# A recommendation tower on one core: wider warm-up products, a wait moved, transposes regrouped and five gather holds removed

## The reference, cut to what matters

```python
e = stack([tbl_f[ids[:, f]] for f in range(26)], axis=1)      # 512 samples, 26 tables, 128 floats a row
combined = concatenate((dense[:, None, :], e), axis=1)         # 27 slots a sample
inter = einsum('bfd,bgd->bfg', combined, combined)             # 27 x 27 products a sample
z = concatenate((dense, inter[:, iu, ju]), axis=1)             # 351 pairs above the diagonal
h = concatenate([z, dense], axis=1)                            # 607 columns
h = maximum(h @ W_top1 + b_top1, 0)                            # 512
h = maximum(h @ W_top2 + b_top2, 0)                            # 256
y = h @ W_top3                                                 # 1 number a sample
```

## Time and profile before

| | |
|---|---|
| Median of 3 runs | 124.61 us (124.29 to 125.33) |
| Span of the profiled execution, first to last instruction | 123.0 us |
| The profiled execution's own time | not given apart from its span; the median is 1.6 us above the span |
| PE busy, PEld busy | 104.2 us, 87.9 us |
| VectorE, ScalarE, GpSimd busy | 65.4, 48.1, 65.7 us |
| DMA | 13.51 MB, mean 110 GB/s |
| Chain that ended last | PE 83%, "issue" 13%, VectorE 2%, ScalarE 1% |

### The profile page before, as it was taken

One profiled execution on the slowest core, in us unless ns is written; L12 is line 12 of the kernel. 1 busy time (PEld: TensorE's weight loads), 2 busy tenths in 40 slices (PEclk: granted clock), 3 DMA queues, 4 the chain that ended last, 5 costly groups with the idle time before them and its releaser, 6 DMA issues.

```text
span 123.0 us, 3436 instructions
## 1 busy us (share of the span) xinstructions
PE 104.2 (85%) x1516; PEld 87.9 (71%) x1516; DVE 65.4 (53%) x110; ACT 48.1 (39%) x81; POOL 65.7 (53%) x66
## 2 busy tenths in 40 slices
PE   6999999999999999962178996289995299998993
PEld 6787888888888888831067895177992278996991
DVE  2599999999899996820001742105540106451411
ACT  4542979197794931300000462002541102730321
POOL 3887888579878887877500887503778305000000
PEclk9999999999999999999555999756999558999999
DMA  3799999999211112121200111200112100000000
GB/s 57 236 400 365 402 398 408 410 392 368 80 43 45 45 43 48 44 63 43 64 5 5 43 43 43 64 0 0 45 43 64 43 0 20 23 0 0 0 0 1
DMA packets 3949, 13.51 MB, mean 110 GB/s; under 512 B 1315, under 2 KB 1317, under 8 KB 3302
## 3 DMA queue, kind: packets, MB, share of 16 engines
q1 hardware_dynamic: 2018, 9.48, 20.5%
q0 software_dynamic: 1920, 3.94, 11.2%
q10 hardware_dynamic: 4, 0.00, 0.0%
HBM read 13.42 MB, written 0.00 MB: 109 GB/s over the span
## 4 chain that ended last, share of the span: by engine, by line
PE 83%; issue 13%; DVE 2%; ACT 1%
PE bank L365 17%; PE prod L408 13%; PE bank L414 13%; PE prod L365 12%; PE bank L374 7%; PE bank L504 6%; PE prod L433 4%; PE bank L321 4%; PE bank L325 3%; PE bank L445 2%; DVE inter_s L585 1%; PE bank L438 1%; PE prod L421 1%; PE bank L421 0%; DVE xT L575 0%
## 5 line engine op out<-in xcount | busy, mean ns | idle before, releaser
L313 POOL DMA_INDIRECT emb<-in_tbl,ids_sb x60 | 65.0, 1083 | 38.3 <-PE prod L408 19.3
L522 DVE TENSOR_SCALAR mask<-ids_h,ids_sb 128x1024 fp32r<-128x1024 int16 (+1 forms) x48 | 31.5, 699 | 2.2 <-issue 0.8
L408 PE MATMUL prod<-xT 128*27 128x27 f32 x1024 | 16.8, 215 | 14.7 <-issue 14.2
L408 PEld LDWEIGHTS prod<-xT 128*27 128x27 f32 x1024 | 13.6, 128 | 18.8 <-issue 17.4
L585 DVE STREAM_TRANSPOSE inter_s<-prod 128x288 f32<-128x288 f32 (+1 forms) x8 | 4.6, 611 | 26.3 <-PE prod L408 26.3
L365 PE MATMUL bank<-mask,high 128*128 128x512 f32 x46 | 15.2, 393 | 0.0
L365 PE MATMUL bank<-mask,low 128*128 128x512 f32 x46 | 15.0, 390 | 0.0
L414 PE MATMUL bank<-pairs,w_sb 117*128 117x128 f32 x96 | 12.7, 282 | 0.1
L414 PEld LDWEIGHTS bank<-pairs,w_sb 117*128 117x128 f32 x96 | 11.6, 191 | 0.7 <-ACT pairs L696 0.5
L531 DVE TENSOR_TENSOR low<-table,high 128x1024 fp32r<-128x1024 f32 (+1 forms) x9 | 11.7, 1301 | 0.0
L374 PE MATMUL bank<-ident,emb 128*128 128x128 f32 x60 | 10.5, 310 | 0.9 <-issue 0.9
(11 more groups left out here) (55 smaller groups left out, 118.1 us busy)
## 6 DMA issues: line engine op xcount, KB each, us to landing
table<-in_resident SPq DMA_DIRECT2D x3, 1024.0 KB
w_sb<-in_weights SPq DMA_DIRECT2D x1, 1792.0 KB
table<-in_resident SPq DMA_DIRECT2D x1, 1280.0 KB
table<-in_resident SPq DMA_DIRECT2D x4, 256.0 KB
emb<-in_tbl,ids_sb POOLq DMA_INDIRECT x60
ids_h<-in_other_ids SPq DMA_DIRECT2D x1, 896.0 KB
table<-in_resident SPq DMA_DIRECT2D x1, 640.0 KB
ids_h<-in_pair_ids SPq DMA_DIRECT2D x1, 256.0 KB
```

The lines of the kernel that those rows point to most:

```text
L313: nc.gpsimd.indirect_dma_start(out=rows(t, c), out_offset=None, in_=gathered[c], in_offset=bass.IndirectOffsetOnAxis(ap=ids_sb[:, i:i + 1] ...
L408: mm = nc.tensor.matmul(prod[SLOT_PITCH * q:SLOT_PITCH * q + SLOTS, i, 0:SLOTS], x, x, start=True, stop=True)
L522: nc.vector.tensor_scalar(made(step)[:, 0:n, :], ids_h[:, 2 * b:2 * b + n, :], col_sb[:, row:row + 1], None, ALU.is_equal).then_inc(s_mask, 1)
```

## The change

- `keep_busy` multiplies 128 columns instead of 64, and its second use has 5 calls instead of 7.
- A semaphore `s_warmed` is counted behind that second use, and ScalarE's cast of pair 1 waits for it instead of for `s_used` at 1.
- Between the halves of the products TensorE transposes groups 0 and 1 of the next tile. The dense parts 0 and 1 stand behind the second half in every pass, pass 1 too; nothing else stands there.
- The five holds of GpSimd behind the lookups are gone: before gather 10 of tile 2 and before gathers 0, 4, 9 and 13 of tile 3 (counted from 0). The four holds within the lookups stay, and the waits for the buffers (`s_tr`).

```diff
-WARM_UP, WARM_KEEP = 4, 7
-WARM_COLUMNS = 64
+WARM_UP, WARM_KEEP = 4, 5
+WARM_COLUMNS = 128
@@
+        s_warmed = sem("s_warmed")
@@ hold
                 if (t, i) == (2, 6):
                     pool.wait_ge(s_used, first_step[5] + 3)
-                if (t, i) == (2, 10):
-                    pool.wait_ge(s_prod, 1)
-                if (t, i) == (3, 0):
-                    pool.wait_ge(s_l1, 2)
-                if (t, i) == (3, 4):
-                    pool.wait_ge(s_prod, 2)
-                if (t, i) == (3, 9):
-                    pool.wait_ge(s_l1, 4)
-                if (t, i) == (3, 13):
-                    pool.wait_ge(s_prod, 3)
@@
             def keep_busy(n):
                 for _ in range(n):
-                    nc.tensor.matmul(half_bank[1][:, 0:WARM_COLUMNS], warm, warm[:, 0:WARM_COLUMNS], start=True, stop=True)
+                    mm = nc.tensor.matmul(half_bank[1][:, 0:WARM_COLUMNS], warm, warm[:, 0:WARM_COLUMNS],
+                                          start=True, stop=True)
+                return mm
@@
-            keep_busy(WARM_KEEP)
+            keep_busy(WARM_KEEP).then_inc(s_warmed, 1)
             look_up_first()
@@ the tile loop
                 products(range(MATMULS // 2))
-                turn_next(p, (0,))
-                with nc.tensor.If(p < 2):
-                    dense_part(slice(0, P), (0, 1))
+                turn_next(p, (0, 1))
                 products(range(MATMULS // 2, MATMULS)).then_inc(s_prod, 1)
                 samples = bass.ds((p - 1) * P, P)
                 with nc.tensor.If(p > 1):
 
                     result(p - 1)
-                    dense_part(samples, (0, 1))
-                turn_next(p, (1,))
+                dense_part(samples, (0, 1))
@@ upper_parts
-                    act.wait_ge(s_used, 1)
+                    act.wait_ge(s_warmed, 1)
```

## The result

The changed kernel takes 139.59 us (median of 6 runs, 137.93 to 140.25) against 124.79 us for the kernel before beside it (6 runs, 124.29 to 125.33): ratio 1.112, 95% interval 1.106 to 1.118. It is slower by 15 us. The profiled execution has a span of 138.1 us and took 139.92. Every median here is over all executions of a kernel, but every ratio compares only executions outside a second, slower state that any kernel falls into now and then, so a ratio can differ by some tenths of a per cent from that of the two medians beside it.

A forecast was written before the change was run, and what follows sets the result against it. TensorE was taken to bound it nearly throughout, starved 17.3 us beside gathers. 100.3 + 38.7 - 5.5 - 0.9 = 132.6 us span, plus 1.6 for the median, 134.2, said as 134; range 121 to 139.

The forecast's parts named there:

- Gathers starve TensorE: Products of passes 1 to 3: gathers cause the starved stretches, 17.3 us, argued from three gather ends just before TensorE's return.
- The order of events: Pass 1's first half starves to 67 or 68 us, its second stretches, pass 2's first starves, pass 3 doesn't.
- the late effect: Rival: starvation begins only some time after a restart, so pass 1's second half escapes; span 126.5, forecast 128; chance 0.11.
- the faster case: Rival: held gathers' bursts starve passes 2 and 3, so only pass 1 pays; span 117, forecast 118.5; chance 0.20.
- no change: Rival: the stretches belong to the loop, not the gathers; 123 to 125 us, forecast 124; chance 0.13.
- The reserve: Beside gathers TensorE has 50 matmuls at full rate before creeping, refilled when gathers pause; in pass 1's second half, 19 left.
- the upper bound, +3 to +5: If the reserve counts from the gathers' issue, pass 1's second half waits out all eight gathers: +3 to +5 us.
- The return: Pass 1's first half: TensorE returns at 67.7 us, after the last gather's end at 65.9.
- The front: Start of the lookups: wider products raise the clock before the first lookup matmul, pair 0 ends at 14.5, gain 1.2 us.
- the allowance: Lookups: alongside gathers TensorE can steadily issue 4.0 matmuls a us; the lookups need 4.4 and were said to fit.
- The low clock: Layer 1 after pass 1's products takes 1 us more at the low level; two turned groups between halves 2.05 us.
- The sum: Span 132.6 us, +9.6: pass 2's products end at 100.3, plus 38.7, minus 5.5 and 0.9 saved in pass 3 and later.

The follow-up runs named there:

- run 6: The kernel before without the 26 gathers from gather 4 of tile 2 on: 106.21 us against 125.72.
- run 7: The kernel before with the same 26 loads as plain transfers of fixed rows from GpSimd's queue: 104.63 us against 125.72, ratio 0.831.
- run 8: The kernel before with the same 26 loads as plain transfers from SyncE's queue, behind the same holds: 105.58 us against 125.72.
- run 9: The kernel before with the 26 gathers replaced by fills of an unread tile on GpSimd, no transfer: 106.04 us against 125.72.
- run 5: The changed kernel once more, unaltered, beside the kernel before on another occasion: 106.78 us against 106.92, ratio 1.003.
- run 3: The kernel before with only the wider products of ones and the cast's new wait: 106.01 us against 106.85, ratio 0.994.
- run 2: The changed kernel with its five holds put back: 106.04 us against 106.85 for the kernel before, ratio 0.992.
- run 10: The kernel before with wider products of ones, the cast's new wait and three holds instead of five: 105.86 us against 107.09, ratio 0.993.
- run 12: The changed kernel with its five holds put back, once more: 106.21 us against 107.09 for the kernel before, ratio 0.995.

## Why the prediction was right, and where it was not

**The cause.** Gathers starve TensorE: right. It rested on three ends that came together; runs 6 to 9 show it, and narrow it to gathers by index. I had not asked whether it holds always. It doesn't: in three of five occasions the same kernels show a small part of it (0.6 to 0.9 us a half), and the change costs nothing there (run 5). The one trace that I had could not have told me. What makes an occasion a starving one is open; every execution here is a recorded one, and records of several engines and of the transfers go missing on just these occasions, in the lookups as well. So it may be the recording itself that gets in TensorE's way beside gathers, and then the kernel would not lose this time without it. No run could tell that apart.

**The order of events.** Right piece by piece: both halves of pass 1 and the first half of pass 2 starve, pass 3 does not. The eight gathers that group 1's early turn admits run from 71.78 to 81.45 beside the second half of pass 1. The rivals fall on this trace: the late effect (that half would have taken 1.7 us; it took 11.65), the faster case (pass 2's first half would have been at full rate; it took 9.15), no change.

**The reserve.** This is the step that was off most. I took 50 matmuls and let the count begin with the gathers' data, 1.6 us behind the issue. The size fits this trace: 45 matmuls go at full rate from 72.30 to 72.90. But the start does not: the first gather is issued at 71.78 and TensorE is starved from 72.9, while the first byte of that gather moves only at 73.4. So in this trace TensorE starves before any data of these gathers flow; what starves it first is not their moving. 83 matmuls were left then instead of 19. 38 of them crept through in 10.3 us, 3.7 a us, and the rest waited for the gathers' end. The second half took 11.65 us instead of 8.9. I had named this as the upper bound, +3 to +5. The sum also has a small slip here: the middle of its own 5 to 9 us gives 79.0 for the end of that half and not 79.5.

**The return.** The gathers of tile 2 ended at 65.90, as forecast (65.9). I let TensorE return 1.8 us later; it took 3.0, to 68.95. With the matmuls then left, the second half began 1.8 us later than forecast (72.36 against 70.6).

**The front.** Forecast -1.2, and +0.1 came. At the start the lead is there: TensorE's first six lookup matmuls took 1.87 us instead of 2.67 in the chain,

```profile
6.74 1.87 PE bank L312 x6
8.62 1.36 PE bank L316 x6
...
15.15 0.44 PE bank L365 x4
```

pair 0 ended at 15.15 (forecast 14.5, before 16.10), and the lookups' last matmul began at 52.20 instead of 52.85. That is 0.31 us for each of the six and not the 0.23 forecast, and it is no steady effect of the wider products: the group of these six is busy for 2.22 us here and 2.32 in run 3, but for 2.95 to 3.00 in runs 2, 5, 10 and 12, which have the same wide products, against 2.91 in the kernel before. Nor do the clock's rows bear out my reading of that stretch: between 4 and 11 us the granted clock stands at 1.00 in both kernels, while the first six matmuls of the kernel before take 0.45 us each. What sets their length there is open.

The rest of the lead is lost at the lookups' end. The products wait for VectorE's copy of the last table, and the copy waits for TensorE's last count (before, then after):

```profile
53.28 0.37 DVE L575 COPY xT<-bank 128x128 f32<-128x128 f32 x1 [1.52 <-PE bank L365]
...
53.37 0.37 DVE L565 COPY xT<-bank 128x128 f32<-128x128 f32 x1 [2.27 <-PE bank L356]
```

Before, the copy starts 0.04 us after the profile's end of the last lookup matmul (53.24); after, 0.78 us after it (52.59). The last counts of `s_used` in the changed kernel's trace come 0.7 us apart (51.91, 52.62, 53.34), although their matmuls are issued 0.45 apart. So what TensorE sends was late already here, beside gathers, and took the lead back. I had written that the lookups live within the allowance; at 4.4 matmuls a us they lie over the 4.0 that I had worked out. The forecast for the cast (worth nothing) was right in its size and wrong in its reason: it waits for its table.

**The low clock.** Forecast 1 us more for the layers of pass 1, and 1.6 came: from the products' end to pass 2 it was 9.4 us (84.01 to 93.39) instead of 7.8. Two cold groups were 1.90 to 1.97 us, against 2.05.

**The sum.** 132.6 against 138.1 of span. Along the path that the sum took, the 5.5 us are: pass 1's first half 1.8 (the late return 1.2 of it), its second half 2.7, its layers at the low clock 0.6, pass 2's products 0.7, and from there on -0.3. The front's missing 1.2 us is not among them, because the sum let the gathers' end and not the front decide when that first half ends. The measured median lies just over the range's upper end, 139; taken by its ratio to the 124.61 us that I had, it is 138.6. The range was wide, and the measured loss of 15 us is over one and a half times the 9.6 forecast: the mechanism was right and its size too small.

**The Trainium skill's rule on branches** (Runtime: NRT & Kernel Launch, "Instruction fetch mechanics") would have left the stretches where they were. Run 6 keeps every branch of the loop and has none of the stretches, so they are not of that kind. Nor does the rule's case arise in them: by the starts of the instruction packets (run 6) nothing is fetched in the starved stretches of the kernel before. What may be a fetch's share is the pause of 0.26 to 1.09 us in pass 1's second half.

**A version that beats both.** None is shown beyond the 0.6 and 0.7% of runs 3 and 10, on occasions without starvation. On a starving occasion the runs without these gathers are 15 to 17% below the kernel before by the medians, but they leave out lookups that the result needs.

## What to carry to other kernels

Where an engine stands at "issue" and nobody is named, look at what the other queues were doing at each end of the stretch, and ask whether the stretch follows their work or the loop. In these runs gathers by index are not free to an engine that issues small matmuls fast; beside the 512-column matmuls of the lookups they cost little. So keep waits that look idle until it is shown what they keep apart. And time before and after on more than one occasion: here the same change is 11% slower on one and nothing on another.

## What the runs showed of the hardware that I had not expected

- The kernel before takes 125 us on two occasions (124.79, 125.72) and 107 us on three (106.85, 106.92, 107.09), on one chip both, with TensorE's issue beside gathers as the difference, as the two traces of the changed kernel show (stretches of 7.6 to 14.6 us, or halves of 1.8 to 2.1).
- Beside gathers by index, where it starves, TensorE issues 1.2 and 2.2 matmuls a us in the first half of pass 1 (18 in 14.6 us, before 17 in 7.9) and 2.8 to 3.7 in the later stretches; beside plain transfers from the same GpSimd queue it runs at full rate (128 in 1.27 us).
- A starved stretch outlasts the last gather by 1.3 to 3.0 us, and it can begin before a gather's first byte moves (72.9 against 73.4 us in the changed kernel). In pass 1 the last byte moves at 67.0 and TensorE is back at 68.95.
- On a starving occasion records of semaphore counts are lost for TensorE (40 of 52), VectorE (31 of 48) and the transfers (530 arrivals against 1129), while no matmul's record is.
- A plain 64 KB transfer costs GpSimd 0.55 us, a gather of as many bytes by index 1.25.
